# Where the bias of a graph convolution is added: by VectorE after the 1/deg scaling, or by TensorE into the operand of the product

## The reference

```
x1  = layernorm(x + adj @ (exp(-evals*t)[:, None] * (adj.T @ x)))       # spectral part
hat = adj + eye(N);  deg = sum(hat, axis=1)
h   = tanh((hat / deg) @ (x1 @ W) + b)                                   # graph convolution
out = layernorm(x1 + h)
```

## Time and profile before

| | |
|---|---|
| Time, median of 3 runs | 679.38 us (674.29 to 680.82) |
| The profiled execution's own time | 677.96 us |
| Its span in the trace | 676.1 us |
| Mean granted clock of PE | 0.964 of full |
| Busy: PE / DVE / POOL / ACT | 626.0 / 519.4 / 363.7 / 405.4 us |

### The profile page before, as it was taken

How to read it: one execution, slowest core, us unless ns; L and a number is a source line. 1 busy time by engine, 2 the same in 40 slices (tenths; PEclk the granted TensorE clock), 3 DMA queues, 4 the chain that set the end, 5 groups by cost and what they waited for, 6 DMA issues and landing times.

```text
span 676.1 us, 8253 instructions
## 1 busy us (share of the span) xinstructions
PE 626.0 (93%) x2584; PEld 473.7 (70%) x2584; DVE 519.4 (77%) x591; ACT 405.4 (60%) x886; POOL 363.7 (54%) x190
## 2 busy tenths in 40 slices
PE   3999999999966899989999999999999997999993
PEld 2888777877754566758877777878878875656561
DVE  3898988899788985775979749757766657479982
ACT  5998999999777344344555536544454432426664
POOL 0000000000417876486999779959779755648782
PEclk9999999999996998988999979999999999999997
DMA  8999999999997997659964589906399709999202
GB/s 287 387 386 386 387 387 387 387 386 387 359 315 192 279 274 198 180 140 227 298 183 114 151 201 303 259 0 180 108 218 320 201 1 268 347 270 347 58 17 62
DMA packets 132842, 166.30 MB, mean 246 GB/s; under 512 B 6596, under 2 KB 96964, under 8 KB 132808
## 3 DMA queue, kind: packets, MB, share of 16 engines
q1 hardware_dynamic: 84752, 117.48, 54.9%
q10 hardware_dynamic: 48056, 48.39, 26.6%
HBM read 163.74 MB, written 2.11 MB: 245 GB/s over the span
## 4 chain that ended last, share of the span: by engine, by line
PE 72%; DVE 8%; DMA 7%; POOL 6%; ACT 4%; issue 2%; ACTq 1%; SPq 0%; POOLq 0%; DVEq 0%
PE ps L752 12%; PE ps L754 11%; PE ps L753 11%; PE ps L728 8%; PE ps L730 7%; PE ps L729 7%; PE ps L748 7%; DMA raw<-in_adj_dram 7%; POOL lo L412 4%; DVE vt L599 4%; PE ps L819 2%; PE ps L818 2%; PE ps L824 2%; ACT hi L445 1%; PE ps L821 1%
## 5 line engine op out<-in xcount | busy, mean ns | idle before, releaser
L412 POOL TENSOR_TENSOR lo<-vt,hi 128x1024 fp32r<-128x1024 f32 x129 | 329.6, 2579 | 100.6 <-ACT hi L460 99.8
L599 DVE STREAM_TRANSPOSE vt<-raw 128x1024 f32<-128x1024 f32 x184 | 222.6, 1229 | 104.5 <-PE ps L754 70.7
L460 ACT ACTIVATE hi<-vt 128x1024 fp32r<-128x1024 f32 x166 | 173.8, 1061 | 151.1 <-DVE vt L599 127.5
L582 DVE TENSOR_TENSOR lo<-raw,hi 128x1024 fp32r<-128x1024 f32 x124 | 153.4, 1239 | 22.3 <-ACT hi L445 20.9
L445 ACT ACTIVATE hi<-raw 128x512 fp32r<-128x512 f32 x256 | 158.3, 622 | 14.5 <-DMA raw<-in_adj_dram 6.0
L752 PE MATMUL ps<-hi,s_hi 128*128 128x512 f32 x232 | 100.2, 432 | 12.2 <-POOL lo L412 10.6
L728 PE MATMUL ps<-hi,xg_hi 128*128 128x512 f32 x256 | 102.7, 401 | 8.7 <-DVE lo L582 7.3
L395 POOL TENSOR_TENSOR lo<-raw,hi 128x1024 fp32r<-128x1024 f32 x4 | 10.7, 2671 | 180.8 <-ACT hi L445 180.8
L730 PE MATMUL ps<-hi,xg_lo 128*128 128x512 f32 x256 | 100.5, 393 | 0.0
L729 PE MATMUL ps<-lo,xg_hi 128*128 128x512 f32 x256 | 100.5, 392 | 0.0
L752 PE MATMUL ps<-hi,p_hi 128*128 128x512 f32 x212 | 90.7, 428 | 7.4 <-POOL lo L412 7.0
(11 more groups left out here) (66 smaller groups left out, 561.6 us busy)
## 6 DMA issues: line engine op xcount, KB each, us to landing
raw<-in_adj_dram SPq DMA_DIRECT2D x64, 1024.0 KB, 14.2
raw<-in_adj_dram SPq DMA_DIRECT2D x80, 512.0 KB, 9.3
raw<-in_adj_dram ACTq DMA_DIRECT2D x80, 512.0 KB, 10.4
late_raw<-in_adj_dram SPq DMA_DIRECT2D x8, 512.0 KB, 13.2
late_raw<-in_adj_dram ACTq DMA_DIRECT2D x8, 512.0 KB, 14.4
xn<-in_x_dram SPq DMA_DIRECT2D x8, 256.0 KB, 12.4
x_sb<-in_x_dram SPq DMA_DIRECT2D x8, 256.0 KB, 11.9
out_dram<-x_sb ACTq DMA_DIRECT2D x8, 256.0 KB, 2.8
```

The source lines that it names most:

```text
L412: nc.gpsimd.tensor_tensor(lo[:, slot(p), :], vt[:, slot(p), :], hi[:, slot(p), :].bitcast(f32), ALU.subtract).then_inc(pool_lo_ready, 1)
L460: nc.scalar.activation(hi[:, slot(s), :], vt[:, slot(s), :], ACT.Copy).then_inc(hi_ready, 1)
L582: nc.vector.tensor_tensor(lo[:, q % RING1, :], raw[:, k, 2 * h:2 * h + 2, :].rearrange("p r n -> p (r n)"), hi[:, q % RING1, :].bitcast(f3 ...
L599: nc.vector.transpose(vt[:, slot(s), :].rearrange("p (m a i) -> p m a i", m=2, a=RB), load_buffer(st.load).rearrange("p (a m e i) -> p e m ...
```

## The change

b leaves p. The eight products with one row in each block (lines 819 and 824), the row of ones, its memset and two waits ahead of PE's loop are gone. In stage 3, VectorE gets four new instructions for each row, one for each 128 columns, that compute sum x 1/deg + b in PSUM, two positions behind the group's end; ScalarE's tanh then has one scale for all columns, and is one instruction of 512 instead of four of 128. It waits for VectorE instead of PE.

```diff
@@ ScalarE, ending3
                 if since == 3:
-                    act.wait_ge(sumT_done, row + 1)
-                    act.wait_ge(deg_in, 16 * NG)
-                    for r in range(R):
-                        last = nc.scalar.activation(acc[:, r * C:(r + 1) * C], acc[:, r * C:(r + 1) * C], ACT.Tanh,
-                                                    scale=rdeg[:, g, r:r + 1])
-                    last.then_inc(tanh_ready, 1)
+                    act.wait_ge(pre3, row + 1)
+                    nc.scalar.activation(acc, acc, ACT.Tanh).then_inc(tanh_ready, 1)
@@ VectorE, ending3
                 acc = acc3(g, NG)
+                if since == 2:
+                    dve.wait_ge(sumT_done, row + 1)
+                    dve.wait_ge(deg_in, 16 * NG)
+                    for r in range(R):
+                        last = nc.vector.scalar_tensor_tensor(
+                            out=acc[:, r * C:(r + 1) * C], in0=acc[:, r * C:(r + 1) * C],
+                            scalar=rdeg[:, g, r:r + 1], in1=b_bc[:, :], op0=ALU.mult, op1=ALU.add)
+                    last.then_inc(pre3, 1)
@@ TensorE, ending2
                     for m in range(JB):
-                        out_t = acc2(g)[:, m * C:(m + 1) * C]
-                        nc.tensor.matmul(out_t, stage[:, 1, m * P:(m + 1) * P], w_sb[:, :], start=True, stop=False)
-                        nc.tensor.matmul(out_t, ones[:, :], b_bc[:1, :], start=False, stop=True)
+                        nc.tensor.matmul(acc2(g)[:, m * C:(m + 1) * C], stage[:, 1, m * P:(m + 1) * P], w_sb[:, :],
+                                         start=True, stop=True)
 
                     nc.tensor.matmul(acc3(g, g), w_sb[:, :], stage[:, 1, :].rearrange("c (m q i) -> c q m i", m=JB, q=QN),
-                                     start=g == 0, stop=False)
-                    for m in range(JB):
-                        last = nc.tensor.matmul(acc3(g, g)[:, m * P:(m + 1) * P], b_bc[:1, :], ones[:, :],
-                                                start=False, stop=False)
-                    last.then_inc(xw_done, 1)
+                                     start=g == 0, stop=False).then_inc(xw_done, 1)
```

More of the change, by code:

```diff
@@ L241, in spectral_then_graph_conv @@
         saves = sb("saves", [P, 2, CW])
-        ones = sb("ones", [1, P])
         ident = sb("ident", [P, P])
@@ L281, in spectral_then_graph_conv @@
         stored = sem("stored")
-        ident0, ident_ready, mhalf_ready, eps_ready, ones_ready = map(
-            sem, ("ident0", "ident_ready", "mhalf_ready", "eps_ready", "ones_ready"))
+        ident0, ident_ready, mhalf_ready, eps_ready = map(sem, ("ident0", "ident_ready", "mhalf_ready", "eps_ready"))
         negt_ready, ev_turned, evT_done, coef_ready = map(sem, ("negt_ready", "ev_turned", "evT_done", "coef_ready"))
@@ L293, in spectral_then_graph_conv @@
             sem, ("x1T_done", "x1T_ready", "xw_done", "phi_ready", "p_ready", "saved"))
-        deg_s, sum3, sumT_done, tanh_ready, y_ready = map(
-            sem, ("deg_s", "sum3", "sumT_done", "tanh_ready", "y_ready"))
+        deg_s, sum3, sumT_done, pre3, tanh_ready, y_ready = map(
+            sem, ("deg_s", "sum3", "sumT_done", "pre3", "tanh_ready", "y_ready"))
         st3, mv3, ag3, ve3, pw3, rs3, out_ready = map(sem, ("st3", "mv3", "ag3", "ve3", "pw3", "rs3", "out_ready"))
@@ L387, in _ @@
             nc.gpsimd.memset(eps_sb[:, :], EPS).then_inc(eps_ready, 1)
-            nc.gpsimd.memset(ones[:, :], 1.0).then_inc(ones_ready, 1)
             pool.wait_ge(mhalf_ready, 1)
@@ L694, in ending3 @@
                     mean_and_var(par, row, st3, ag3, mv3)
+            dve.wait_ge(b_in, 16)
             for p in range(AHEAD, POSITIONS):
@@ L836, in _ @@
             pe.wait_ge(w_in, 16)
-            pe.wait_ge(b_in, 16)
-            pe.wait_ge(ones_ready, 1)
             for p in range(AHEAD, POSITIONS):
```

## The result

The changed kernel took 647.74 us (median of 4 runs, 642.36 to 648.98), the kernel before, run beside it, 677.07 us (4 runs, 674.29 to 680.82): a ratio of 0.955, with an interval of 0.947 to 0.963. The profiled execution of the changed kernel took 648.07 us, its span is 645.9 us, 30.2 less than before; the sum of the prediction was 24.6.

What follows compares the result with a forecast made beforehand. PE was taken as the bound, with little room before GpSimd and VectorE; 22.1 - 2 + 6 - 2 + 0.5 = 24.6 us off 677.96 gives 653.4, set at 654 us; range 644 to 666, the forecast's own 649 to 657.

Steps and rivals of the forecast that it cites:

- The bias products: Eight one-row products in each of eight PE blocks, at full clock: 2.76 us a block, 22.1 us gained.
- The clock: Half-clock stretches (falls) in or behind four PE blocks: most go, 8 of 11.9 us less 2, so 6 us gained.
- What is held back: At the blocks, 2 us taken off for group 2's busy GpSimd and loads freed early; part of the clock's 11.9 too.
- VectorE in stage 3: New VectorE instructions: 1.13 us for a row's four, 9.0 for eight rows, 2 us lost on the path (0 to 4.5).
- all 9.0 us would be paid: Stage 3 by the skill page's rule on a saturated VectorE: full cost paid, sum 17.6 us instead of 24.6.
- The tail: Last row's chain from transposes to L690: with one tanh of 512 columns, L690 comes 0.5 us earlier.
- The falls stay: Rival at PE's blocks: the clock falls behind the remaining short products as before; 660 us, chance 0.20.
- The helpers bind: Rival: GpSimd and VectorE take the first four blocks' gain, and no clock gain passes; 669 us, chance 0.13.
- All passes: Rival: the falls go and stage 3 hides VectorE's work, 33.5 us gained; 645 us, chance 0.08.
- The slower one: Rival in stage 3: each new VectorE instruction stands behind GpSimd, 9.0 us a row, half hidden; 688 us, chance 0.04.

Runs made afterwards that it cites:

- the long full rows: The full-row kernel (bias products of 128 rows) with each bias product doubled by one on zeros; one execution, 673.27 us.
- two wide rows: The kernel before with two one-row bias products of 512 columns in each block instead of eight of 128; 661.1 us, ratio 0.968.
- full rows: The kernel before with all its bias products in the same places, but with 128 rows instead of one; 654.98 us, ratio 0.958.
- VectorE's part alone: The changed kernel with the eight one-row products kept in each block, on a row of zeros; 676.81 us, ratio 0.995 to the kernel before.

## Why the prediction held, and where it missed

**The forecast of 654 us** stood for "blocks shorter, most falls gone, some held back, stage 3 about neutral", and that is what happened; 647.74 lies in the range of 644 to 666, just under the forecast's own 649 to 657.

**The bias products: the term that was too small.** The step that failed is "the products L818 that stay could follow each other at the 0.31 us between the first two starts or at 0.42 as later; I take 0.42, which gives nothing beyond". They follow at 0.22, and the block lost 3.72 us, not 2.76: 8 x 3.72 = 29.8 instead of 22.1. I priced the eight products by their own distances to the next start, which held five changes of kind (one for each L819, one for the four L824), and left their neighbours' part, 10 x 0.193 - 5 x 0.193 = 0.97 us a block, in the kernel that stays. The rows had it: L818 at 0.42 beside 0.31 at the block's head, and L821 at 1.06 for two passes.

**The clock: direction right, value of the right size.** I took 11.9 nominal, less 2 for a fall that stays or comes up elsewhere, so 9.9; measured it is 8.5 (27.2 to 10.2 us at half clock). The four falls behind blocks went, two came up behind waits. The prediction's "the rows have PE busy ahead of the fall" is right for groups 0, 3 and 7; ahead of group 1's block PE had waited 0.98 us. That the falls need the alternating one-row products and not the length of the block is what the long full rows show, in one profile. Booking 6 of the 9.9 us was cautious rather than high: with two wide rows and with full rows some 9 us of 10.2 and of 11.9 came through.

**What is held back.** I took off 2 us, and another 3.9 of the clock's gain, 5.9 in all; measured against blocks and clock together it is 6.2. The difference of the stretch is then 32.1 - 26.1 = 6.0 = 7.7 (blocks) - 1.4 (clock) - 0.3 (held back). The places are those named: the loads "whose buffer was freed ahead of a block", and GpSimd, from step 27 to 103. PE's waits for GpSimd's `lo` between 300 and 400 us rose from 0.8 us (as much as the earlier trace rows has for 330 to 560) to 2.4 and 4.1 in the two profiles. I had not seen `p_lo` behind VectorE's `lo`.

**VectorE in stage 3.** Four instructions in 1.14 us, as taken from L637 (1.13); 0.5 to 1.6 us on the path, where I took 2. The page "Perfetto Trace Analysis", Optimizing Scalar/DVE Operations, of the Trainium skill says that with a saturated VectorE it may make sense to move work to ScalarE, and gives no price; that all 9.0 us would be paid was my reading of it. The run of VectorE's part alone, at 0.995 (0.991 to 1.000) where 9 us are 1.3%, excludes that.

**The tail**, the chain in order of time in the changed kernel:

```profile
634.65 0.77 PE ps L829 x4
...
635.44 1.14 DVE ps L685 x4
...
636.62 0.59 ACT ps L531
...
637.24 0.71 DVE ps L691
```

From the transposes' start to the addition of x1 it is 637.24 - 634.65 = 2.59 us, where the earlier trace rows have 667.41 - 664.24 = 3.17: 0.6 earlier, for 0.5 predicted, by the steps that were named.

**The rivals.** "The falls stay" (660) is refuted: none stands behind a block. "The helpers bind" (669) is partly true: from step 27 to 103 4.8 us of 21.7 are held back, and there loads are likely to have at least as much of it. "All passes" (645; its own terms add up to 34.0 us and not 33.5) came nearest in time, but for another reason than it gave: about 6 us are held back, and shorter blocks make up for them. That the time fell so near its figure is luck. The slower one is refuted by the 0.36 us of the longest new instruction.

## What to carry to other kernels

A short product's price is read against the same product without its neighbour: a one-row product between 128-row ones here cost more by its two changes of kind (0.39 us) than by its passes (0.22), and filling its rows up, at no cost in passes, brought most of what taking it away did. Half of the time that the bounding engine spends at half clock is a fair first price of it, even where the engines behind it are nearly full: some 9 us of 10.2 and of 11.9 came through here, and the one pair of profiles that said 1.2 of 6.8 stood against the others. An engine at 87% can still take work, where another is the bound and a ring of several steps lies between them.

## What the runs showed of the hardware that was not expected

- Going over between products of one row and of 128 rows costs PE about 0.19 us each way (block of 5.47 us with ten changes, 3.54 with none and the same passes; one inserted product 0.61 us, its passes 0.22).
- The granted clock fell to 1.2 GHz in or behind 4 and 3 of 8 blocks with such changes, for five of these seven with PE busy for all of the 3.40 us ahead, and behind none of 8 blocks of 5.32 us with 128 rows throughout.
- The new instruction, which reads PSUM, a tile of SBUF and a per-partition scalar, stayed at 0.32 to 0.36 us beside GpSimd's `lo`; VectorE's `lo`, which reads two tiles of SBUF, went from 1.18 to as much as 3.37 us.
